# Edge sorts of a four-layer graph network: one-hots tile by tile, counts summed within four tiles, second ranks scattered later

## What is computed

```python
edge_index = jnp.stack([src, dst])            # 103125 edges
h = jnp.maximum(_layernorm(x), 0.0); x = x + _L0_gnn_ref(h, ...)   # 3 hops of attention, softmax over edges by src
h = jnp.maximum(_layernorm(x), 0.0); x = x + _L1_gnn_ref(h, ...)   # 3 layers of graph attention, 4 heads, softmax by dst
h = jnp.maximum(_layernorm(x), 0.0); x = x + _L2_gnn_ref(h, ...)   # 2 graph convolutions and 2 dense layers
h = jnp.maximum(_layernorm(x), 0.0); x = x + _L3_gnn_ref(h, ...)   # attention over src + relation, softmax by dst
```

## Time and profile before

| what | value |
|---|---|
| median of three runs | 9573.84 us (9569.98 to 9581.71) |
| the profiled execution | 9577.8 us, its span 9575.8 us |
| busy share of the span | TensorE 67%, weight loads 54%, VectorE 76%, ScalarE 58%, GpSimd 66% |
| L245, payload scatters of sort 0 | 816, 843.1 us |
| L1871, payload scatters of sort 1 | 816, 1657.0 us |
| L296, lookup products | 3264, 755.6 us |
| L406 and L409, one-hots | 408 each, 277.4 and 102.3 us |
| L337 and L454, ranks | 38 and 12, 112.6 and 42.5 us |
| L445, scans | 50, 88.0 us |
| L498 and L345, first slots added | 2 and 12, 32.6 and 21.6 us |

### The profile page before, as it was taken

How to read it: one execution, slowest core, us unless ns; L and a number is a source line. 1 busy time by engine, 2 the same in 40 slices (tenths; PEclk the granted TensorE clock), 3 DMA queues, 4 the chain that set the end, 5 groups by cost and what they waited for, 6 DMA issues and landing times. The chain is left out here.

```text
span 9575.8 us, 217005 instructions
## 1 busy us (share of the span) xinstructions
PE 6368.2 (67%) x63738; PEld 5150.9 (54%) x63739; DVE 7308.4 (76%) x20527; ACT 5592.6 (58%) x12073; POOL 6322.6 (66%) x5522
## 2 busy tenths in 40 slices
PE   3894796555555565546655478878878869467775
PEld 2893796444444444434444355555555544366665
DVE  9779777667777577766777799989989970388886
ACT  4224325546665566656666489979979950144443
POOL 0777773067776777767777578858858850377776
PEclk8555555678887788877788799999999989788887
DMA  0210114622222222222222222212212237232322
GB/s 12 65 53 2 59 61 139 232 48 52 53 52 42 52 52 52 52 43 51 52 52 52 48 56 56 56 50 56 57 42 62 56 93 280 76 53 54 54 54 50
DMA packets 411419, 617.79 MB, mean 65 GB/s; under 512 B 267559, under 2 KB 324353, under 8 KB 387609
## 3 DMA queue, kind: packets, MB, share of 16 engines
q0 software_dynamic: 185232, 370.99, 16.7%
q1 hardware_dynamic: 158592, 160.26, 5.4%
q10 hardware_dynamic: 67497, 85.32, 2.5%
HBM read 513.10 MB, written 104.66 MB: 65 GB/s over the span
## 5 line engine op out<-in xcount | busy, mean ns | idle before, releaser
L914 POOL DMA_INDIRECT l_land<-table,l_words x3504 | 3377.2, 964 | 1115.1 <-issue 1066.6
L1871 POOL DMA_INDIRECT ell<-gat_stage_pay,gat_stage_at x816 | 1657.0, 2031 | 261.8 <-issue 248.4
L1506 PE MATMUL left_product_ps<-k_w,messageT 128*128 128x128 f32 x5136 | 882.4, 324 | 670.8 <-ACT messageT L1541 670.8
L1506 PEld LDWEIGHTS left_product_ps<-k_w,messageT 128*128 128x128 f32 x5136 | 740.9, 222 | 850.3 <-ACT messageT L1541 850.3
L1966 ACT COPY gat_probT<-gat_ps 128x512 f32<-128x512 f32 (+1 forms) x2100 | 1017.2, 552 | 71.6 <-PE gat_ps L1911 62.8
L245 POOL DMA_INDIRECT ell<-pay,position x816 | 843.1, 1033 | 289.3 <-issue 280.0
L1557 ACT ACTIVATE weighed<-kept,l_prob 128x128 f32 x3120 | 988.2, 390 | 68.6 <-ACT l_prob L1059 68.6
L1059 ACT ACTIVATE l_prob<-l_shifted,l_fall 128x9 f32<-128x9 f32 x506 | 153.3, 303 | 1493.5 <-DVE l_fall L1053 1485.5
L2429 PE MATMUL rel_ps<-relation_parts,hot 128*128 128x128 bf16 x11328 | 789.2, 241 | 338.7 <-DVE hot L2530 338.3
L2429 PEld LDWEIGHTS rel_ps<-relation_parts,hot 128*128 128x128 bf16 x11328 | 766.5, 110 | 361.6 <-DVE hot L2530 361.5
L296 PE MATMUL looked_ps<-count,loT_wide 128*128 (+1 forms) x3264 | 755.6, 384 | 47.5 <-issue 44.3
(11 more groups left out here) (351 smaller groups left out, 14927.2 us busy)
## 6 DMA issues: line engine op xcount, KB each, us to landing
gcn_edges<-counts SPq DMA_DIRECT2D x50, 1600.0 KB, 8.0
l_land<-table,l_words POOLq DMA_INDIRECT x3504
rows<-low_dram SPq DMA_DIRECT2D x34, 1536.0 KB
counts<-pair_turned_sb ACTq DMA_DIRECT2D x12, 3200.0 KB
logs<-pair_logs ACTq DMA_DIRECT2D x12, 3200.0 KB, 18.2
ell<-pay,position POOLq DMA_INDIRECT x816
ell<-gat_stage_pay,gat_stage_at POOLq DMA_INDIRECT x816
l_words<-ell SPq DMA_DIRECT2D x446, 8.0 KB
```

The costliest lines, as they stand in the source:

```text
L914: pool.indirect_dma_start(self.land[:, p, s, :], None, table[:, :], bass.IndirectOffsetOnAxis(ap=self.words[:, p, s, 0:1], axis=0)).then_i ...
L1506: mm = pe.matmul(right_ps[:, k * H + j, :], messageT[:, k, j, :], k_w[:, :], start=True, stop=True)
L1871: pool.indirect_dma_start(c.ells[1][:, :], bass.IndirectOffsetOnAxis(ap=stage_at[n % 2][:, t:t + 1], axis=0), stage_pay[n % 2][:, t, :], N ...
```

## The change

- One-hots: eight tiles a step and two buffers. `lo_hot` is made by eight instructions of 128x128, one a tile, that take the key as a scalar from memory; `hi_now` by one of 128x200, with the keys as bf16 (`hi_b`).
- Counts: TensorE no longer sums degrees. The product of tile j goes to the counts of tiles j to 3 of its group of four, so that `count` holds sums within four tiles. Products per tile fall from two to one, with 25 to 100 columns.
- Scans: only the 204 totals of the groups are scanned, into `base`, and the degrees are read off the end of it. The scans now stand ahead of the degrees.
- Ranks: VectorE does 12 blocks, ScalarE 13.
- First slots are added to `base` (204 x 25) instead of `count`. `place` adds `base` to a chunk's counts; the first chunk's before the lookup, each later one's in round 1 of the chunk before it. TensorE waits for `places_ready` at each chunk.
- No scatters for the ten pad tiles, in either sort.
- The 25 scatters of sort 1's ranks move into the first layer of `graph_attention`, one behind each read of the logs; list and degrees are read back at its end.

```diff
-    NV = 6
-    NA = 19
+    NV = 12
+    TURN = ST // 2
+    RUNS, RUN = TL // H, CT // H
@@ gpsimd @@
-                for t in range(k * CT, (k + 1) * CT):
+                for t in range(k * CT, min((k + 1) * CT, z.filled)):
...
-            rank_nodes(1)
-            pool.wait_ge(placed, 16 * TL)
+            pool.wait_ge(placed, 16 * z.filled)
@@ tensor @@
-                        for j in range(H):
-                            pe.matmul(degree_ps[:, :], lo_hot[:, h, j, :], hi_now[:, h, j, :], start=False, stop=False)
-                            mm = pe.matmul(counts_ps[h][:, j, :], lo_hot[:, h, j, :], hi_now[:, h, j, :],
-                                           start=True, stop=True)
+                        for j in range(S):
+                            here = j % H
+                            mm = pe.matmul(counts_ps[k][:, j:j - here + H, :], lo_hot[:, k, j, :],
+                                           spread(hi_now[:, k, j, :], [P, H - here, NB], 1),
+                                           start=(here == 0), stop=(here == H - 1))
...
-                pe.wait_ge(places_ready, 2 * q + 2)
...
                 def matches(k, last):
+                    pe.wait_ge(places_ready, k + (q * CH + 1))
@@ scalar @@
-                act.wait_ge(first_ready, q + 1)
-                for b in range(NA, NB):
-                    last = nc.scalar.activation(count[:, 0:TL, b], count[:, 0:TL, b], ACT.Identity,
-                                                bias=first_slot[:, b:b + 1])
-                last.then_inc(places_ready, 1)
@@ vector @@
+                V.tensor_copy(hi_b[:, :], part_i[:, :])
...
+                def hots(k, i):
+                    first = i * (2 * S) + k * S
+                    for j in range(S):
+                        V.tensor_scalar(lo_hot[:, k, j, :], iota_rb[:, :], lo_f[:, bass.ds(first + j, 1)], None, ALU.is_equal)
+                    V.tensor_tensor(hi_now[:, k, :, :], spread(iota_rb[:, 0:NB], [P, S, NB], 1),
+                                    spread(hi_b[:, bass.ds(first, S)], [P, S, NB], 2),
+                                    ALU.is_equal).then_inc(hots_ready[k], 1)
...
-                v.wait_ge(degree_ready, q + 1)
-                step(V.tensor_copy(deg, degree_ps[:, :]))
+                for k in range(2):
+                    v.wait_ge(counts_kept[k], 1 + (q + 1) * TURN)
+                by_run = count[:, 0:TL, :].rearrange("p (s j) n -> p s j n", j=H)
+                for b in range(NB):
+                    V.tensor_tensor_scan(base[:, :, b], by_run[:, :, 0, b], zero[:, 0:1].to_broadcast([P, RUNS]), 0.0,
+                                         ALU.add, ALU.add)
+                v.drain()
+                step(V.tensor_tensor(deg, base[:, RUNS - 1, :], count[:, TL, :], ALU.add))
...
-                V.tensor_tensor(count[:, 0:TL, 0:NA], count[:, 0:TL, 0:NA], spread(first_slot[:, 0:NA], [P, TL, NA], 1),
-                                ALU.add).then_inc(places_ready, 1)
+                step(V.tensor_tensor(base[:, :, :], base[:, :, :], spread(first_slot[:, :], [P, RUNS, NB], 1), ALU.add))
+
+                def place(at, run_at):
+                    here = count[:, bass.ds(at, CT), :].rearrange("p (s j) n -> p s j n", j=H)
+                    begun = base[:, bass.ds(run_at, RUN), :]
+                    V.tensor_tensor(here[:, :, 1:H, :], here[:, :, 1:H, :], spread(begun, [P, RUN, H - 1, NB], 2), ALU.add)
+                    V.tensor_copy(here[:, :, 0, :], begun).then_inc(places_ready, 1)
+
+                place(0, 0)
...
                         add(r, tile)
+                        if r == 1 and not last:
+                            place(k * CT + CT, k * RUN + RUN)
...
-                v.wait_ge(perm_in, 16 * (q + 1))
-                V.tensor_copy(c.degs[q][:, :], c.perms[q][:, :, 1])
+                if not q:
+                    v.wait_ge(perm_in, 16)
+                    V.tensor_copy(c.degs[0][:, :], c.perms[0][:, :, 1])
@@ graph_attention @@
-    PART = -(-z.tiles // PARTS)
-    starts = [n * z.tiles // PARTS for n in range(PARTS + 1)]
+    PART = -(-z.filled // PARTS)
+    starts = [n * z.filled // PARTS for n in range(PARTS + 1)]
...
+                        if not layer:
+                            pool.indirect_dma_start(c.perm_dram[1][:, :],
+                                                    bass.IndirectOffsetOnAxis(ap=c.late_rank[:, i:i + 1], axis=0),
+                                                    c.late_pairs[:, i, :], None).then_inc(late_out, 16)
```

## The result

The changed kernel takes 9636.7 us (median of five runs, 9623.4 to 9647.7); the kernel before took 9577.6 us beside it (9570.0 to 9581.7). The ratio is 1.0059, 95% interval 1.0048 to 1.0069: slower by 59 us, where 25 were forecast. The profiled execution has a span of 9634.9 us against 9575.8.

The account below looks back on a forecast made before the run. VectorE bounds one-hots, the serial stretch and graph attention, TensorE the lookup at 1.2 GHz. 9 + 12 + 1 - 35 + 29 - 1.5 + 11 = +25 us on the 9573.8 median gives 9599 us; range 9548 to 9640.

Parts of the forecast that it names:

- Slower was forecast as likeliest: Whole kernel: slower by over 0.2% at chance 0.54, faster 0.17, the rest 0.29.
- the six cases: Whole kernel: the forecast's numbered outcomes with their chances, from 9493 us to 9690 us.
- case 4: Whole kernel: the forecast itself holds, slower, 9592 to 9615 us; chance 0.42.
- case 5: One-hots of the sorts: VectorE's sequencer is the bound, 0.22 us an instruction, 9645 to 9690 us; chance 0.11.
- One-hots: Both sorts: eight small instructions and a compare take 1.595 us against 1.55 for eight tiles; 9 us lost.
- Both rivals for that row: 128x128 tensor-scalar: 0.10 us if the scalar costs nothing extra (chance 0.07), 0.22 if the sequencer is the bound (0.11).
- GpSimd beside them: Second sort's one-hots: each of 111 GpSimd issues delays VectorE's small instructions 0.10 us; about 12 us lost.
- Between the stretches: From one-hots to lookup: scans add 12.7 us, ranks win 20.9, first slots 9.4; -17.6 us a sort, -35 for both.
- Places in the lookup: Lookups: 1.23 us of added VectorE work a chunk less 0.33 slack costs TensorE 0.90 us; 29 us over 32 chunks.
- Layer 0: Graph attention's first layer: late rank scatters overfill GpSimd; 11 us lost over the last 12 blocks, bounds 0 and 25.
- the named wait: Graph attention's first layer: VectorE waits for reads of the logs from about the twelfth block, in sum 11 us.
- What leaves the sort: Sort's end: pad and second-rank scatters on GpSimd were hidden behind VectorE; 1.5 us won, 0 to 4.

## Why the prediction was right and wrong

**Sign and size.** Slower was forecast as likeliest, and the time lies in the range, near its upper end. The terms that the forecast named sum to +7.9 in the sorts and +12.4 in layer 0, 20 us for the 25 forecast. 39 of the 59 us have no term in it. That 20 comes near 25 is in part luck, since the one-hots came 15 us under their terms and the lookups 10 over. That the time lies in the range is luck too: none of the six cases covers 9636.7 us, case 4 ends at 9615 and case 5 begins at 9645, and what lifted the time that far has no place in the sum.

**One-hots: right.** 0.165 us were forecast and 0.163 measured for a 128x128 tensor-scalar with its scalar from memory, 1.595 and 1.58 for eight tiles. Both rivals for that row fall, 0.10 and 0.22 us. The Trainium skill, page "VectorE: DVE Perf Modes", has a table in its section on the TRN2 errata by which, as an estimate, it would be 94 ns; the measurement decides for 163. The warning of the same section, that small operations on SBUF pay a fixed latency, is borne out: 0.13 of the 0.163 us is fixed by the forecast's split, and one compare of 1024 elements, at 1.14 us, wins over eight small ones at 1.30.

**GpSimd beside them: wrong, 12 us too many.** The 0.10 us by which four 128x512 instructions differed was carried over to every issue. It doesn't carry: +3.7 in sort 1, +3.6 in sort 0. The Trainium skill, page "SBUF — State Buffer", section "Who interferes with whom", has the two exclude each other for whole instructions. For these small ones the trace doesn't show it: some last longer, up to 0.50 us, but it hardly delays the next. The `low` one-hot of 128x512 (L527 before) is held up at times: of its 408 instructions in the kernel before 49 take 0.43 to 0.58 us, all beside an issue, while 330 others beside an issue take at most 0.36.

**Between the stretches: right.** -17.6 forecast, -18.0 and -17.4 measured. A scan takes 0.48 us from start to start for 0.49, twelve ranks end at 240.0, the base add takes 5.47 us for 5.4. (The recorded 9.4 us for the first slots should be 16.3 - 5.4 - 1.3 = 9.6.)

**Places in the lookup: mechanism right, the added work too small.** The forecast had 1.23 us of added work and 0.33 us of slack, 0.90 us lost a chunk; 1.21 were measured. Where TensorE waits for the mask, its weights come 0.88 to 0.89 us behind it; what lies between mask and weights beyond that is slack. In the kernel before, the round in which the places will stand looks like this in two chunks (`loT`, the `low` one-hot; the next mask; TensorE's weights):

```profile
335.47 0.58 DVE L527 TENSOR_SCALAR loT<-rows,iota_col 128x512 bf16 x1
...
336.41 0.68 DVE L533 TENSOR_TENSOR matched_at<-match_ps,earlier 128x512 bf16<-128x512 f32 x1
...
337.38 1.83 PEld L296 LDWEIGHTS looked_ps<-count,loT_wide 128*128 128x128 f32 x8
...
363.28 0.34 DVE L527 TENSOR_SCALAR loT<-rows,iota_col 128x512 bf16 x1
...
363.97 0.68 DVE L533 TENSOR_TENSOR matched_at<-match_ps,earlier 128x512 bf16<-128x512 f32 x1
...
365.17 1.83 PEld L296 LDWEIGHTS looked_ps<-count,loT_wide 128*128 128x128 f32 x8
```

From mask to weights it is 0.97 us in the first, with a slow one-hot ahead, and 1.20 in the second. One chunk misleads: over the 32 chunks that are followed by another in their sort the mean is 1.16 us, and only two have 0.97. So the slack was 0.28 us, near the forecast's 0.33. What the forecast had too small is the work. From mask to mask this round takes 3.85 us in the changed kernel and 2.37 in the one before (means over the 32 chunks), 1.48 us more, and the block itself is 1.29 of it. Its surroundings in the second of these chunks, in the changed kernel:

```profile
352.36 0.54 DVE L517 TENSOR_SCALAR loT<-rows,iota_col 128x512 bf16 x1
353.09 0.26 DVE L532 TENSOR_REDUCE found<-picked 128x100 f32 x1 [0.18 <-issue]
353.35 1.10 DVE L486 TENSOR_TENSOR count<-count,base  x1
```

The one-hot ahead takes 0.45 us or more in 25 of the 32 chunks, 0.51 on average, for 5 chunks and 0.38 before; and the block follows the sum (`found`) after 0.26 us, where the mask did after 0.17. Then 1.48 - 0.28 = 1.20 us a chunk, 38 us; 38.8 were measured. Why the one-hot is held up beside GpSimd's issues so much more often there is not shown.

**Layer 0: right by the sum, with less of it in the named wait.** 11 forecast, 12.4 measured; putting the scatters back gave 9.5. The wait for the logs shows only 7.4 us; VectorE's waits for TensorE on L2038 in this layer rose from 6.1 to 9.9 us. The forecast also slipped in its own count: if some ten of 25 blocks pass before the slack is gone, 15 are left and not 12, which makes 14 us. The layers without any added issue lost too, 7.9 and 4.5 us, and had no term. For layer 2 no cause in the change is needed, since the kernel with 300 unused bytes is 5.2 us longer there as well. The 7.9 us of layer 1 are not in that kernel (1.3 us) and stay open. TensorE stops in these layers once in a while for 1 to 3 us with no wait that the profile shows:

```profile
6650.01 0.11 PEld L1917 LDWEIGHTS gat_ps<-gat_probT,h 128*32 128x32 f32 x1 [2.44 <-issue]
...
6651.22 0.13 PEld L1917 LDWEIGHTS gat_ps<-gat_probT,h 128*32 128x32 f32 x1 [1.11 <-issue]
```

Such stops of over 1 us, without the one of 18 us as each layer begins, are not the change's: layers 1 and 2 have nine in the changed kernel and one in the kernel before, but nine also in the kernel with 300 bytes, and layer 0 has five in the kernel before.

**The untouched 3500 us: not in the forecast at all.** "What leaves the sort" was costed; what later code would feel of it was not. 12 of the 28 us went away with idle increments in the five streams, so they hang on where code stands in some stream; which one is not shown, and the other 16 are open.

## What to carry to other kernels

Read slack over all chunks, at the round in which the added work will stand: single chunks gave 0.09 and 0.32 us here, the mean was 0.28. Add to the work what it does to its neighbours, here 0.19 us on 1.29. Cut added work into pieces smaller than the idle time of one round before moving it anywhere; the same additions cost 1.2 us a chunk in one block and 0.2 us in five (6.5 us over 32 chunks). And before a change of a few tenths of a per cent is put down to its mechanism, time the kernel with a few idle instructions put in: here 80 of them took 12 us out of a stage that they don't touch, and ten casts of some 7 us made the kernel 18 us longer.

## What the runs showed of the hardware

- Idle instructions aren't neutral: with 80 semaphore increments ahead of it the first attention took 3531.7 us for 3544.0, and VectorE was busy in its unchanged loops for 2537 us instead of 2567.
- Two of the chips ran the kernel before in 12.7 to 12.9 ms instead of 9.57. On these VectorE stands still for up to 31 us at a time, while GpSimd goes on issuing a scatter every 1.27 us (24 of them in the longest stop). From the waits of VectorE in the first lookup of the kernel with ten casts, and its timeline there:

```profile
DVE picked L538 <- remote: 710.3, 48, 30.8
```

```profile
422.00 0.96 POOL L245 DMA_INDIRECT ell<-pay,position  x1 [0.31 <-issue]
422.31 0.69 DVE L533 TENSOR_TENSOR matched_at<-match_ps,earlier 128x512 bf16<-128x512 f32 x1 [3.81 <-remote]
423.26 0.96 POOL L245 DMA_INDIRECT ell<-pay,position  x1 [0.30 <-issue]
424.53 0.96 POOL L245 DMA_INDIRECT ell<-pay,position  x1 [0.30 <-issue]
```

The lookup of sort 0, with 785 scatters issued beside it, lasts 1383 us there for 469. That of sort 1 lasts 487 us for 468, with 17 issues beside it (on the other chip 344). The cause of these stops is open.
